# A transformer decoder on one core: threshold search of expert choice, first row load and up products of the routed experts rewritten

## The reference

```python
logits = flat @ gate_w
scores = softmax(logits) + gate_b
_, topi = top_k(scores, 2)
weights = take_along_axis(logits, topi)
capacity = ceil(2048 * 2 / 16 * 1.25)            # 320
def per_expert(gid, w1, w3, w2):
    assigned = (topi == gid).any(-1)
    wm = where(assigned, w_tok, -inf)             # w_tok: this token's logit for the expert
    vals, idx = top_k(wm, capacity)               # an expert keeps its 320 best tokens
    y = (silu(flat[idx] @ w1) * (flat[idx] @ w3)) @ w2 * where(assigned[idx], vals, 0)[:, None]
    return idx, y
out = zeros.at[idxs].add(ys) + mean of two shared experts on all tokens
```

## Time and profile before

| what | value |
|---|---|
| median of 3 executions | 1380.44 us (1379.09 to 1383.38) |
| profiled execution, its own time | 1377.93 us |
| its span, first to last instruction | 1376.0 us |
| PE busy | 1247.9 us, 91% |
| DVE busy | 980.6 us, 71% |
| ACT busy | 710.2 us, 52% |
| POOL busy | 622.6 us, 45% |
| mean granted clock of PE | 0.957 |
| chain that ended last | PE 67%, DVE 16%, ACT 5%, issue 4%, POOL 4% |

### The profile page before, as it was taken

How to read it: one execution, slowest core, us unless ns; L and a number is a source line. 1 busy time by engine, 2 the same in 40 slices (tenths; PEclk the granted TensorE clock), 3 DMA queues, 4 the chain that set the end, 5 groups by cost and what they waited for, 6 DMA issues and landing times.

```text
span 1376.0 us, 29293 instructions
## 1 busy us (share of the span) xinstructions
PE 1247.9 (91%) x10862; PEld 913.7 (66%) x10862; DVE 980.6 (71%) x2360; ACT 710.2 (52%) x1471; POOL 622.6 (45%) x770
## 2 busy tenths in 40 slices
PE   7999999999999989842669989989999999989998
PEld 5667667667776756530347656767777777777887
DVE  5988897787788778678313467677878888776554
ACT  4566666666666646510113345556666666633222
POOL 3555555555555521120631368685555755401110
PEclk9999999999999999965879989999999999999999
DMA  5131000000000020000023134211120211000001
GB/s 179 55 124 32 1 2 1 1 1 1 1 1 1 1 70 2 1 1 0 11 65 98 37 73 119 41 49 30 38 57 20 56 38 29 4 1 1 0 0 30
DMA packets 77000, 43.87 MB, mean 32 GB/s; under 512 B 26090, under 2 KB 71739, under 8 KB 76871
## 3 DMA queue, kind: packets, MB, share of 16 engines
q1 hardware_dynamic: 72390, 38.58, 10.6%
q10 hardware_dynamic: 2432, 2.28, 0.5%
q0 software_dynamic: 2048, 1.27, 0.4%
HBM read 21.89 MB, written 10.49 MB: 24 GB/s over the span
## 4 chain that ended last, share of the span: by engine, by line
PE 67%; DVE 16%; ACT 5%; issue 4%; POOL 4%; SPq 2%; DMA 1%; POOLq 0%; DVEq 0%; ACTq 0%
PE psum L1670 8%; PE psum L1270 7%; PE psum L1779 6%; PE psum L1255 6%; PE psum L1245 6%; PE psum L1790 4%; PE psum L1682 4%; PE psum L1654 4%; PE psum L1661 3%; PE psum L1502 3%; ACT arena L895 2%; PE psum L1221 2%; POOL xs_rows L666 2%; PE psum L1512 2%; DVE arena L2187 2%
## 5 line engine op out<-in xcount | busy, mean ns | idle before, releaser
L614 POOL TENSOR_TENSOR arena<-arena,rden 128x512 f32<-128x512 f32 x256 | 260.6, 1042 | 215.1 <-DVE rden L1925 215.0
L895 ACT ACTIVATE arena<-psum,negmax 128x512 f32<-128x512 f32 x256 | 175.1, 694 | 151.0 <-DVE negmax L1916 124.1
L2458 DVE TENSOR_REDUCE negmax<-psum 128x1 f32<-128x512 f32 x256 | 164.6, 685 | 50.4 <-PE psum L1661 48.3
L1916 DVE TENSOR_REDUCE negmax<-psum 128x1 f32<-128x512 f32 x256 | 168.1, 681 | 40.2 <-PE psum L1245 39.0
L1255 PEld LDWEIGHTS psum<-cst,arena 128*128 128x128 f32 x1024 | 112.6, 141 | 47.4 <-issue 46.8
L1255 PE MATMUL psum<-cst,arena 128*128 128x128 f32 x1024 | 139.3, 277 | 4.4 <-DVE arena L1911 0.8
L1245 PE MATMUL psum<-a_qk 64*128 64x512 f32 x768 | 106.1, 408 | 2.5 <-DVE a_qk L1934 2.5
L1779 PE MATMUL psum<-f_h,f_w 128*128 128x512 f32 x384 | 100.3, 410 | 7.1 <-DVE arena L2556 6.9
L1654 PE MATMUL psum<-a_kstack,a_qblk 96*128 96x512 f32 x256 | 96.9, 460 | 9.9 <-DMA a_kstack<-a_klo 7.4
L1149 ACT ACTIVATE arena<-psum 128x512 f32<-128x512 f32 x64 | 38.1, 597 | 107.5 <-PE psum L1779 107.5
L1245 PEld LDWEIGHTS psum<-a_qk 64*128 64x128 f32 x768 | 67.2, 184 | 39.1 <-issue 24.2
(11 more groups left out here) (342 smaller groups left out, 2722.3 us busy)
## 6 DMA issues: line engine op xcount, KB each, us to landing
w<-in_ew SPq DMA_DIRECT2D x2, 2048.0 KB, 9.5
a_kstack<-a_khi SPq DMA_DIRECT2D x64, 64.0 KB, 2.0
xs_rows<-f SPq DMA_DIRECT2D x3, 1024.0 KB, 5.3
arena<-xs_rows SPq DMA_DIRECT2D x8, 384.0 KB, 3.7
ys_rows<-wqkv SPq DMA_DIRECT2D x8, 384.0 KB, 2.6
a_kstack<-a_klo SPq DMA_DIRECT2D x32, 64.0 KB, 2.0
a_kstack<-a_khi SPq DMA_DIRECT2D x64, 32.0 KB, 1.9
a_qstack<-a_qhi SPq DMA_DIRECT2D x121, 16.0 KB, 2.7
```

What stands on the lines that cost most here:

```text
L614: pool.tensor_tensor(a0_p[u % 4], a0_p[u % 4], rden[:, u:u + 1].broadcast_to([P, SEQ]), ALU.mult).then_inc(a0_norm, 1)
L895: act.activation(a0_p[u % 4], bank[u % 4][:, :], ACT.Exp, bias=negmax[:, u:u + 1], accum_out=den[:, u:u + 1]).then_inc(a0_exp, 1)
L1916: dve.tensor_reduce(negmax[:, u:u + 1], bank[u % 4][:, :], AX.X, ALU.max, negate=True).then_inc(a0_max, 1)
L2458: dve.tensor_reduce(negmax[:, n % 8:n % 8 + 1], bank[n % 4][:, :], AX.X, ALU.max, negate=True).then_inc(a1_max, 1)
```

## The change

Three parts, in one edit.

The search keeps the tries, not the bounds. The first bound is a power of two taken from the exponent of the maximum, all 16 steps are made ahead of the rounds from a row of constants, and the three tries of the next round come in one instruction from the number of full ones, the step, and a base `g_from` that was made from the round's lowest try while PE counts. Both bounds are taken from all tries after the rounds.

The rows of expert 0 and of expert 1 are loaded by DMAs of their own (the first on the semaphore `x0_ones`).

The up products of the routed experts are made from high and low parts, three fp32r products for one f32 product. POOL makes the parts of the weights for all 16 experts (a product with ones and a subtraction instead of a copy, and written out instead of in a loop), DVE those of the rows.

```diff
...
@@ -70,6 +72,10 @@
     c[p, C_HH + p % (HQ * HD) // HD] = 1.0
+    c[:, C_ST:C_ST + BISECT] = 0.5 * float(CUTS + 1) ** -np.arange(BISECT)
+    c[:, C_AT:C_AT + CUTS] = np.arange(1, CUTS + 1) / (CUTS + 1.0) - 1.0
+    c[:, C_AT + CUTS:C_AT + 2 * CUTS] = np.arange(1, CUTS + 1) * 0.5 - 1.0
+    c[:, C_AT + 2 * CUTS:C_AT + 3 * CUTS] = [-1.0] + [1.0] * (CUTS - 1)
     inv = (1.0 / 10000.0 ** (np.arange(0, HD, 2, dtype=np.float32) / HD)).astype(np.float32)
...
@@ -224,6 +231,9 @@
+        w_hi = over("r_whi", [P, 2, 2, FF], "arena", 3 * QT * SEQ)
+        w_lo = over("r_wlo", [P, 2, 2, FF], "qT", 0)
+        assert place["kT"] == place["qT"] + 4 * SEQ and place["vtok"] == place["kT"] + 4 * SEQ
         w13st = arena[:, 3, 0:2, :].rearrange("p e (w f) -> p e w f", w=2)
@@ -245,7 +255,8 @@
         hs = wqkv0[:, 4 * PITCH:8 * PITCH].rearrange("p (e h n) -> p e h n", e=2, h=2)
-        xsT = wqkv0[:, 8 * PITCH:8 * PITCH + 2 * CAP].rearrange("p (e n) -> p e n", e=2)
+        x_hi = over("r_xhi", [P, 2, CAP], "wqkv0", 8 * PITCH)
+        x_lo = [over("r_xlo0", [P, CAP], "hst", 6), over("r_xlo1", [P, CAP], "vtok", 0)]
         g_lg = g_tiles[:, 0, :, :]
...
@@ -514,8 +526,10 @@
             sp.wait_ge(scattered, 16 * 2 * NT)
-            for i in range(2):
-                load_xs(0, i)
+            first_rows = xs_rows.rearrange("(e t p) d -> e p t d", t=ET, p=P)
+            sp.dma_start(xs[:, 0, 0:ET, :], first_rows[0]).then_inc(x0_ones, 16)
+            sp.dma_start(xs[:, 0, ET:, :], first_rows[1]).then_inc(xs_in[0], 16)
+            load_xs(0, 1)
             with sp.Fori(0, E0 // 4 - 1) as j:
@@ -652,8 +666,14 @@
                 pool.memset(gathered[g], 0.0).then_inc(gath_zero, 1)
+
+            def split_up(e):
+                w, high, low = (x.rearrange("p w f -> p (w f)") for x in (w13[:, e, :, :], w_hi[:, e % 2, :, :], w_lo[:, e % 2, :, :]))
+                chained(pool.tensor_tensor(high, w, ones[:, 0:1].broadcast_to((P, 2 * FF)), ALU.mult))
+                pool.tensor_tensor(low, w, high.bitcast(F32), ALU.subtract).then_inc(r_staged, 1)
+
             for e in range(2):
-                pool.tensor_copy(w13st[:, e, :, :], w13[:, e, :, :]).then_inc(r_staged, 1)
+                split_up(e)
             pool.wait_ge(g_pool, 1)
@@ -665,10 +685,9 @@
                                             bounds_check=ROWS - 1, oob_is_err=False).then_inc(scattered, 16)
-            with pool.Fori(1, E0 // 2) as i:
-                for e in range(2):
-                    pool.wait_ge(r_h, i * 4 - 2 + e * 2)
-                    pool.tensor_copy(w13st[:, e, :, :], w13[:, ds(i * 2 + e, 1), :, :].rearrange("p a b c -> p (a b) c")).then_inc(r_staged, 1)
+            for e in range(2, E0):
+                pool.wait_ge(r_h, 2 * e - 2)
+                split_up(e)
@@ -1485,22 +1504,30 @@
             def routed_t(e, k, first):
-                pe.wait_ge(xs_in[k // 2], (e // 4) * 16 + 16)
+                if first and k == 0:
+                    pe.wait_ge(x0_ones, 18)
+                else:
+                    pe.wait_ge(xs_in[k // 2], (e // 4) * 16 + 16)
                 if not (first and k < 2):
-                    pe.wait_ge(r_tc, e - 1)
+                    pe.wait_ge(r_tc, e * 2 - 2)
                 for t in range(ET):
...
             def routed_up(e, k, first):
-                pe.wait_ge(r_tc, e + 1)
+                pe.wait_ge(r_tc, e * 2 + 1)
                 pe.wait_ge(r_staged, e + 1)
...
                     for w in range(2):
-                        mm = pe.matmul(bank[2 * hf + w][:, 0:CAP], w13st[:, k % 2, w, hf * P:(hf + 1) * P], xsT[:, k % 2, :],
-                                       start=True, stop=True)
+                        cols = slice(hf * P, (hf + 1) * P)
+                        o = bank[2 * hf + w][:, 0:CAP]
+                        pe.matmul(o, w_hi[:, k % 2, w, cols], x_hi[:, k % 2, :], start=True, stop=False)
+                        pe.matmul(o, w_lo[:, k % 2, w, cols], x_hi[:, k % 2, :], start=False, stop=False)
+                        if hf == 0 and w == 0:
+                            pe.wait_ge(r_tc, e * 2 + 2)
+                        mm = pe.matmul(o, w_hi[:, k % 2, w, cols], x_lo[k % 2][:, :], start=False, stop=True)
                     mm.then_inc(r_h, 1)
@@ -2137,7 +2164,9 @@
                     dve.wait_ge(r_h, e * 2 - 2)
-                dve.tensor_copy(xsT[:, k % 2, :], bank[4 + k % 2][:, 0:CAP]).then_inc(r_tc, 1)
+                dve.tensor_copy(x_hi[:, k % 2, :], bank[4 + k % 2][:, 0:CAP]).then_inc(r_tc, 1)
+                dve.wait_ge(r_tc, e * 2 + 1)
+                dve.tensor_tensor(x_lo[k % 2][:, :], bank[4 + k % 2][:, 0:CAP], x_hi[:, k % 2, :].bitcast(F32), ALU.subtract).then_inc(r_tc, 1)
@@ -2167,9 +2196,11 @@
-            link(dve.tensor_scalar(g_hi[:, :], g_all[:, :], 1.0 + 2.0 ** -10, 1e-20, ALU.mult, ALU.max))
-            link(dve.tensor_scalar(g_lo[:, :], g_hi[:, :], -1.0, None, ALU.mult))
-            link(dve.tensor_scalar(g_step[:, 0:1], g_hi[:, :], 0.5, None, ALU.mult))
+            link(dve.tensor_scalar(g_hi[:, :].bitcast(I32), g_all[:, :].bitcast(I32), 0x7F800000, None, ALU.bitwise_and))
+            link(dve.tensor_scalar(g_hi[:, :], g_hi[:, :], 2.0, 1e-20, ALU.mult, ALU.max))
+            dve.tensor_scalar(g_step[:, :], steps_from, g_hi[:, :], None, ALU.mult)
+            dve.tensor_scalar(g_try[:, BISECT, :], bounds_from, g_hi[:, :], None, ALU.mult)
+            link(dve.tensor_scalar(g_try[:, 0, :], first_from, g_hi[:, :], None, ALU.mult))
             dve.wait_ge(g_mm, 3)
@@ -2180,20 +2211,23 @@
+            dve.tensor_scalar(g_full[:, BISECT, :], bounds_from, 0.0, None, ALU.is_lt)
             for k in range(BISECT):
-                step, after = g_step[:, k % 2:k % 2 + 1], g_step[:, 1 - k % 2:2 - k % 2]
-                blink(dve.scalar_tensor_tensor(g_try[:, k, :], iota[:, 1:1 + CUTS], step, g_lo[:, :].broadcast_to([P, CUTS]), ALU.mult, ALU.add))
                 for c in range(CUTS):
...
                 ins.then_inc(b_count, 1)
-                blink(dve.tensor_scalar(after, step, 1.0 / (CUTS + 1), None, ALU.mult))
+                step = g_step[:, k:k + 1]
+                blink(dve.scalar_tensor_tensor(g_from[:, :], next_from, step, g_try[:, k, 0:1].broadcast_to([P, CUTS]), ALU.mult, ALU.add))
                 dve.wait_ge(b_total, k + 1)
                 blink(dve.tensor_scalar(g_full[:, k, :], bank[2][:, 0:CUTS], CAP - 0.5, None, ALU.is_ge, ALU.add, g_nfull[:, :]))
-                blink(dve.scalar_tensor_tensor(g_lo[:, :], g_nfull[:, :], step, g_lo[:, :], ALU.mult, ALU.add))
-            link(dve.scalar_tensor_tensor(g_fail[:, :, :], g_full[:, :, :], 1e30, g_try[:, :, :], ALU.mult, ALU.add))
-            link(dve.tensor_reduce(g_low_fail[:, :], g_fail[:, :, :], AX.XY, ALU.min))
+                if k < BISECT - 1:
+                    blink(dve.scalar_tensor_tensor(g_try[:, k + 1, :], g_nfull[:, :].broadcast_to([P, CUTS]), step, g_from[:, :], ALU.mult, ALU.add))
+            link(dve.tensor_scalar(g_full[:, :, :], g_full[:, :, :], 2e30, -1e30, ALU.mult, ALU.add))
+            dve.tensor_tensor(g_low[:, :, :], g_try[:, :, :], g_full[:, :, :], ALU.min)
+            link(dve.tensor_tensor(g_high[:, :, :], g_try[:, :, :], g_full[:, :, :], ALU.max))
+            dve.tensor_reduce(g_lo[:, :], g_low[:, :, :], AX.XY, ALU.max)
             left = upto(80)
-            dve.tensor_tensor(g_hi[:, :], g_hi[:, :], g_low_fail[:, :], ALU.min).then_inc(g_chain, left)
+            dve.tensor_reduce(g_hi[:, :], g_high[:, :, :], AX.XY, ALU.min).then_inc(g_chain, left)
             dve.wait_ge(g_chain, 80)
...
             dve.wait_ge(g_mm, 4)
```

12 lines of the change are left out of this document (8 added, 4 removed).

## The result

The changed kernel took **1371.74 us** (median of 6 runs, 1368.92 to 1374.9), the kernel before in the same comparison 1381.3 us (6 runs, 1379.09 to 1385.97): ratio 0.9937, 95% interval 0.992 to 0.9953. The profiled execution of the changed kernel took 1370.48 us against 1377.93, so 7.45 less; the forecast had 6.4 less, 1374.0 for the median, within 1369 to 1378.

The account below looks back on a forecast made before the run. PE's work was taken to make up two thirds of the bounding chain, with DVE bounding the search. Terms -3.9 + 1.7 + 0 - 4.2 = -6.4 us gave 1374.0 us for the median, range 1369 to 1378.

Parts of the forecast that it names:

- 1. Rounds: Threshold search, 16 rounds: lower bound and next thresholds in one instruction, 2.12 us a round for 2.38; net -3.9 us.
- the head's 0.3: Head of the search: five instructions for three, their 0.3 us counted as hidden while DVE waits for the transposed logits.
- the new end: End of the search: five instructions, three linked, about 1.1 us for 0.75, so +0.35.
- 2. Staging: Softmax string: POOL's products and subtractions for the first two experts hold up two DVE instructions, +1.7 us (bounds 0, 2.4).
- the late maximum: Before the search: POOL's maximum over partitions, behind its splits, ends hidden at 606.3 or about 1 us late; not added.
- 3. First load: Rows of experts 0 and 1 loaded separately: 0 us (bounds -0.5 and +1.0), earlier first half gaining at most 0.22.
- The low part's wait: First routed up products: new wait for the low part of expert 0's rows, 0.2 us.
- 4. Up products: Routed experts: three fp32r products at 150 ns for one f32, 0.53 us a turn, 8 turns, -4.2 us (bounds -6.6, -2.8).
- Products at 136 ns: Rival, routed experts: up products run to their rate, -6.1 us there, sum -8.3, 1372.1 us; chance 0.15.
- No gain from the up products: Rival, routed experts: path through silu and hid bounds a turn, new waits eat the saving; -2.2, 1378.2 us; chance 0.14.
- Exclusion in the routed stretch: Rival, routed experts: POOL and DVE exclude each other, turn 8.8 us for 7.89, sum +5.1, 1385.5 us; chance 0.04.
- The change not doing what it says: Rival, search: round stays at 2.38 us because g_from replaces what was folded; counted within the no-gain rival.

Follow-up runs that it names:

- three moves: Changed kernel with POOL's first two weight splits moved after the scatters (1376.54 us), after the maximum over partitions (1381.09 us), or ahead of the gather-buffer memsets (1378.59 us).
- the splits ahead: Changed kernel with POOL's two first weight splits directly after its layer-norm wait and the gather-buffer memsets after the maximum: 1378.59 us, 0.9949 of the kernel before.
- the load alone: Kernel before with only the first load of rows split in two: 1379.15 us, ratio 0.9981 to the kernel before.

## Why the prediction was right

The time fell inside the range, and each part came within 0.5 us of its term, one of them partly by luck. By its parts, measured against expected:

*1. Rounds,* -4.28 for -3.9, at the bound given. The 0.26 us of the folded instruction was right, sixteen times, and the head's 0.3 was hidden, as assumed. Too dear was the new end, +0.20 where I counted +0.35. And I had read the second round as if all were like it: the eighth took 2.60 us and not 2.38, from compare to compare, in all three traces with the old search, and in none with the new one. That 0.22 us was won without being forecast, and why it was there is open. That g_from "costs nothing" holds only as a difference: it costs the 0.1 us that the step cost before.

*2. Staging,* +1.51 for +1.7. The mechanism is shown: a DVE instruction with two SBUF operands and a POOL product or subtraction reading SBUF hold each other up. It followed the splits into the rounds and vanished when they were moved ahead. The rows of the last stage gave its size. The Trainium skill states it so (SBUF — State Buffer, Who interferes with whom), and adds that the order of issue decides who waits; the 1.22 us of POOL's second rounding product agrees. The other consequence that I named, the late maximum, did come: its record ended at 607.53, and without the hold-up DVE would have asked for it 1.5 us earlier. That is why I was right not to add the two; had the splits not held up the string, the maximum would have been late by an estimated 1.1 us (607.53, less the 0.18 by which POOL was itself held up, against 606.24). Of the two ways in which I let it count, the second is the right one: it starts 5.4 to 6.0 us after POOL's instruction ahead of it in all fourteen traces, but 3.4 to 7.9 us after g_abs. Of the three moves only the splits ahead remove both costs and bring no other: there the maximum ended at 603.32 and was read at 606.26.

*3. First load,* -0.49 for 0, inside its bounds. The wait for the rows, 0.22 us, went as said, and the load alone gave -0.26. The other 0.23 is luck with the clock: in the changed kernel it rose before the third warming product was through (mean 0.74 of full in the half microsecond ahead of the first transpose), in the load alone only behind it (0.50 there). The clock was up when the first up product started (1.00 from 702 on). The low part's wait cost 0.2 us, as counted: the first turn lasts 7.61 us for 7.37, and 6.50 for 6.49 in the kernel that lacks the low part.

*4. Up products,* -4.06 for -4.2: a turn 7.37 with 4.03 of up products, where 7.36 and 4.02 were written. Products of 320 columns start 147 ns apart (ten of them from 747.85 to 749.32), not 150, inside the 145 to 152 that the earlier trace rows gave. With 147 my sum gives 3.96 a turn; the measured 4.03 has 0.07 more in the hand-overs, so two small errors cancel in it. By the estimate of 136 ns from the Trainium skill (TensorE: Matmul & The Clock Gate, Wait — 56ns, not 53.3ns?) it would have been 2 us more, which the 147 ns here rule out.

*The rivals.* Products at 136 ns: no, 147, although the time of that rival, 1372.1 us, lies nearer to the measured 1371.74 than my 1374.0 does. Its reason was misread too: the f32 products do not run at exactly 533 ns, their two records start 269 ns apart, 538 a product. No gain from the up products: no, although a piece of that rival was true, since the path through silu and hid did keep 0.5 us of each turn, as the transposes put between the halves showed. Exclusion in the routed stretch: no, 490 to 494 ns for all 32 hid products. The change not doing what it says: no, 2.13 us a round.

The sum missed by 1.0 us (-7.4 for -6.4), mostly in the search and the load. The medians differ by 9.6, 2 us more than the stretches explain. Only one execution of each has a trace, so where these 2 us lie isn't shown; in the traces the parts that no edit touches move by as much from kernel to kernel.

## What to carry to other kernels

Before work is put on POOL, look at what DVE runs beside it: where its instructions have two SBUF operands they wait for the end of a POOL instruction that reads SBUF, so place POOL's work beside instructions that read PSUM or one operand. Read a change of a few us by stretches, from start to start of the same instructions, and one part at a time; the times of whole runs could not tell -2.5 us from nothing. When products get cheaper, look for the wait that was hidden in them: here it was 0.5 us a turn, and reordering PE's own work removed it.

## What the runs showed that I had not expected

POOL's change from one kind of work to another costs several us in which nothing is recorded: 7.46 us from the last indirect DMA to the first product, 6.72 from the maximum over partitions to the first product, 5.44 to 6.01 from the instruction ahead of the maximum to it, while a memset follows the maximum or an indirect DMA at once. The first two were seen in one trace each, the third in all fourteen. The Trainium skill puts the first call to a freshly loaded kernel at about 6 us, with no instruction in the profile (GPSIMD Engine Reference, Instruction dispatch); the way to the maximum has that size, but no run here shows what is loaded.

The same program can have PE as its bound on one chip where POOL bounds it on another: in the scatter stretch on chip B PE got its last shared products mostly one by one, and the load stretch was 5 to 7 us longer. It was there in all eight kernels run on that chip and in none of the six other traces. Why is open, and with so few chips it can't be told from the time at which the runs were made.
